# Where four bilinear corners are added in 240 of the 576 sampling steps: by VectorE, or by TensorE in accumulating transposes

## The reference

```
val = g00 * (1 - wy1) * (1 - wx1) + g01 * (1 - wy1) * wx1 + g10 * wy1 * (1 - wx1) + g11 * wy1 * wx1
val = val * mask[:, None]
out = jnp.einsum('bckhw,ock->bohw', val, weight.reshape(weight.shape[0], C, KK))
```

## Time and profile before

| what | value |
|---|---|
| median of 3 runs | 8815.93 us (8812.18 to 8817.9) |
| profiled execution, its own time | 8820.57 us |
| its span, first to last instruction | 8818.8 us |
| first gather of iteration 1, 2, 3, and of the final stage | 1375.0, 3312.8, 5248.2, 7175.9 us |
| VectorE busy | 5978.0 us (68%) |
| GpSimd busy | 5508.2 us (62%) |
| TensorE busy | 4891.3 us (55%) |
| ScalarE busy | 2531.7 us (29%) |

### The profile page before, as it was taken

One profiled execution on the slowest core, in us unless ns is written; L12 is line 12 of the kernel. 1 busy time (PEld: TensorE's weight loads), 2 busy tenths in 40 slices (PEclk: granted clock), 3 DMA queues, 4 the chain that ended last, 5 costly groups with the idle time before them and its releaser, 6 DMA issues. The chain is left out here.

```text
span 8818.8 us, 80494 instructions
## 1 busy us (share of the span) xinstructions
PE 4891.3 (55%) x23346; PEld 2932.9 (33%) x23346; DVE 5978.0 (68%) x6782; ACT 2531.7 (29%) x4248; POOL 5508.2 (62%) x5206
## 2 busy tenths in 40 slices
PE   4555675657766556667756566577755632222222
PEld 3333323434433234434433234344433321111111
DVE  5688557778885767778875767788875654444444
ACT  1355331235532312245522312244512300000000
POOL 0000005768877657768877657778877667777776
PEclk9877887778878777778877777788877865555555
DMA  2000033333333543333333533333333533333333
GB/s 77 22 0 0 22 89 110 106 108 91 91 114 107 163 133 102 106 106 90 91 118 107 168 126 105 102 105 90 90 120 106 167 115 112 113 113 113 112 113 104
DMA packets 443193, 887.45 MB, mean 101 GB/s; under 512 B 119073, under 2 KB 268919, under 8 KB 439925
## 3 DMA queue, kind: packets, MB, share of 16 engines
q0 software_dynamic: 248832, 679.81, 26.4%
q1 hardware_dynamic: 190708, 129.65, 5.1%
q10 hardware_dynamic: 3456, 75.50, 2.1%
HBM read 763.04 MB, written 121.53 MB: 100 GB/s over the span
## 5 line engine op out<-in xcount | busy, mean ns | idle before, releaser
L657 POOL DMA_INDIRECT gathered_corners<-gather_table,metas x5184 | 5499.9, 1061 | 3290.0 <-issue 2852.2
L1367 PE MATMUL ps<-ident,sampled 128*128 128x128 f32 (+1 forms) x2160 | 480.8, 375 | 2381.0 <-DVE sampled L745 1273.5
L1124 ACT COPY sampled_by_channel<-ps 128x512 f32<-128x512 f32 x576 | 335.8, 583 | 3370.5 <-PE ps L1367 3130.2
L1444 PE MATMUL ps<-region,woff 128*128 (+2 forms) x3456 | 1232.7, 516 | 23.3 <-ACT region L1109 23.3
L1367 PEld LDWEIGHTS ps<-ident,sampled 128*128 128x128 f32 (+1 forms) x2160 | 319.1, 181 | 2603.0 <-issue 2080.7
L728 DVE TENSOR_TENSOR gathered_corners<-gathered_corners,ps 128x2304 f32<-128x2304 f32 x288 | 735.5, 2554 | 439.4 <-DMA gathered_corners<-gather_table,metas 430.9
L1444 PEld LDWEIGHTS ps<-region,woff 128*128 128x128 f32 x3456 | 689.6, 203 | 521.3 <-issue 100.1
L1351 PE MATMUL ps<-sampled_by_channel,w 128*64 128x256 f32 x2880 | 682.0, 459 | 0.0
L1364 PE MATMUL ps<-ident,weighted_corners 128*128 128x128 f32 (+1 forms) x2880 | 422.8, 313 | 405.5 <-DVE weighted_corners L726 405.5
L739 DVE TENSOR_TENSOR ps<-gathered_corners,ps 128x1152 f32<-128x1152 f32 x144 | 196.2, 1363 | 653.7 <-DMA gathered_corners<-gather_table,metas 652.4
L1364 PEld LDWEIGHTS ps<-ident,weighted_corners 128*128 128x128 f32 (+1 forms) x2880 | 388.3, 158 | 464.7 <-issue 249.5
(11 more groups left out here) (222 smaller groups left out, 8535.2 us busy)
## 6 DMA issues: line engine op xcount, KB each, us to landing
gathered_corners<-gather_table,metas POOLq DMA_INDIRECT x5184
x_after_layer<-region ACTq DMA_DIRECT2D x8, 4608.0 KB, 14.6
gather_table<-tabst SPq DMA_DIRECT2D x192, 192.0 KB
region<-in_x_dram ACTq DMA_DIRECT2D x12, 1536.0 KB, 10.8
region<-x_after_layer ACTq DMA_DIRECT2D x4, 4608.0 KB, 14.7
res<-x_after_layer SPq DMA_DIRECT2D x144, 128.0 KB
out_dram<-ob SPq DMA_DIRECT2D x144, 128.0 KB
indices_and_weights<-region SPq DMA_DIRECT2D x16, 810.0 KB
```

Source lines behind the costliest of these rows:

```text
L657: pool.indirect_dma_start(out=G[:, s % NG, k, :], out_offset=None, in_=table, in_offset=bass.IndirectOffsetOnAxis(ap=idx[:, s * KK + k:s * ...
L1124: nc.scalar.copy(VT[:, i, 0:4, 128 * t2:128 * t2 + 128], ps[:, 5, :].rearrange("p (k n) -> p k n", k=4))
L1367: mm = pe.transpose(out_m, V[:, s % 2, 128 * m:min(128 * m + 128, KK * C)], ident[:, :])
L1444: mm = pe.matmul(out_rows[:, top:bottom, left:right], woff[:, e, k, :], rhs, start=n == 0, stop=n == KK - 1)
```

## The change

In 20 of the 36 groups (0 to 9 and 22 to 31) both engines' `steps_of` lose their argument `False`, so that they take the form with `sum_on_pe`. That is 80 steps in each iteration and 240 in all. The last four groups of an iteration and the final stage keep their forms. The code of the three forms is untouched.

```
-                    steps_of(c, slot, (0,), False, first)
+                    steps_of(c, slot, (0,), first=first)
...
-                    steps_of(c, slot, (2,), False)
+                    steps_of(c, slot, (2,))
...
-                    steps_of(G_NORM, G_NORM % 2, NORM_PLACES.get(c, ()), False)
+                    steps_of(G_NORM, G_NORM % 2, NORM_PLACES.get(c, ()))
...
-                        steps_of(j + G_CONV[0], (j + G_CONV[0]) % 2, CONV_PLACES[e], False)
+                        steps_of(j + G_CONV[0], (j + G_CONV[0]) % 2, CONV_PLACES[e])
...
-                        steps_of(j + G_COSINES, (j + G_COSINES) % 2, COSINE_PLACES[e], False)
+                        steps_of(j + G_COSINES, (j + G_COSINES) % 2, COSINE_PLACES[e])
...
-                    steps_of(c, (0,), False)
+                    steps_of(c, (0,))
...
-                    steps_of(q // 3 + G_CONV[0], CONV_PLACES[q % 3], False)
+                    steps_of(q // 3 + G_CONV[0], CONV_PLACES[q % 3])
```

More of the change, by code:

```diff
@@ L806, in chunk @@
                         ch.named(ch.after().tensor_tensor(ek4[:, i], kps, wide(kmax[:, i]), ALU.subtract), k_sub, c * 2 + (i + 1))
-                    steps_of(c, slot, (1,), False, first)
+                    steps_of(c, slot, (1,), first=first)
                     for i in range(2):
@@ L836, in chunk @@
                             ch.named(ins, at_cp, c + 1)
-                    steps_of(c, slot, (3,), False)
+                    steps_of(c, slot, (3,))
                     if not last:
@@ L864, in _ @@
                 repeat_edges(pad2_1, 2, PAD2)
-                steps_of(G_NORM, G_NORM % 2, (2, 3), False)
+                steps_of(G_NORM, G_NORM % 2, (2, 3))
                 v.wait_ge(x1_stored, 16)
@@ L992, in _ @@
                     for e in range(12):
-                        steps_of(j + G_CONV[1], (j + G_CONV[1]) % 2, SUM_PLACES[e], False)
+                        steps_of(j + G_CONV[1], (j + G_CONV[1]) % 2, SUM_PLACES[e])
                     ch.restart()
@@ L997, in _ @@
                         t = j * 12 + e
-                        steps_of(j + (G_CONV[1] + 2), (j + G_CONV[1]) % 2, SUM_PLACES[e], False)
+                        steps_of(j + (G_CONV[1] + 2), (j + G_CONV[1]) % 2, SUM_PLACES[e])
                         v.wait_ge(c2_mm, t + 1)
@@ L1401, in _ @@
                         mm.then_inc(q_mm, 1)
-                    steps_of(c, (1,), False)
+                    steps_of(c, (1,))
                     for i in range(2):
@@ L1414, in _ @@
                         mm.then_inc(m_mm, 1)
-                    steps_of(c, (2,), False)
+                    steps_of(c, (2,))
                     pe.wait_ge(m_cp, c * 2 + 2)
@@ L1428, in _ @@
                     mm.then_inc(y_mm, 1)
-                    steps_of(c, (3,), False)
+                    steps_of(c, (3,))
                 group_mean(1, oct_avg[:, :])
-                steps_of(G_NORM, (0, 1), False)
+                steps_of(G_NORM, (0, 1))
                 group_mean(2, pair_avg[:, :])
@@ L1460, in _ @@
                     offset_bank(0, 0, b)
-                    steps_of(G_NORM, ((), (2,), (3,), ())[b], False)
+                    steps_of(G_NORM, ((), (2,), (3,), ())[b])
                 for e in range(2):
@@ L1497, in _ @@
                         mm.then_inc(c2_sum, 1)
-                        steps_of(j + G_CONV[1], SUM_PLACES[e], False)
+                        steps_of(j + G_CONV[1], SUM_PLACES[e])
                 pe.wait_ge(c2_copied, RT + 4)
@@ L1505, in _ @@
                                   start=True, stop=True).then_inc(c2_mm, 1)
-                        steps_of(j + (G_CONV[1] + 2), SUM_PLACES[e], False)
+                        steps_of(j + (G_CONV[1] + 2), SUM_PLACES[e])
                 group_mean(4, pair_avg[:, :])
@@ L1524, in _ @@
                         mm.then_inc(n_tr, 1)
-                        steps_of(j + G_COSINES, COSINE_PLACES[tile], False)
+                        steps_of(j + G_COSINES, COSINE_PLACES[tile])
                 pe.wait_ge(cos_cp, RT + 2)
```

## The result

The changed kernel takes 8691.51 us (median of 4 runs, 8684.81 to 8698.38) against 8814.06 us before (4 runs, 8811.01 to 8817.9): a ratio of 0.9865, 95% interval 0.9851 to 0.9878. That is 122.5 us less, where the interval stands for 107 to 131. The forecast was 8685 us, 129 less than 8814, in a range of 8640 to 8750.

What follows compares the result with a forecast made beforehand. GpSimd's gathers were taken as the bound; 104 us from longer gathers, 9 from L817 and 24 from waits sum to 137 us off 8820.6, or 8683.6 us. Allowing for the runs' median and unsure terms it said 8685, range 8640 to 8750.

Steps and rivals of the forecast that it cites:

- What bounds the kernel: GpSimd's gathers are the bound, floor 45.1 us a group of 36; layer 0's nine groups take 432.0 us.
- Longer gathers: Layers 0 to 2 and cosines: gathers no longer held up by VectorE's two-SBUF-operand adds; 34.5 us an iteration, 104 in three.
- L817: Layer 0: this VectorE instruction comes 2.25 us earlier against the gathers; 0.3 us a chunk gained, 9 us over 27 chunks.
- pairs of L730 and L733: The removed VectorE adds, two operands in SBUF, lengthen gathers: 0.44 us a pair in layer 0, 0.4 in the cosines.
- Waits of GpSimd: GpSimd's waits for a free buffer shrink as it is released 2.25 us earlier: 8.0 us an iteration, 24 us.
- so it gives +0.7 to -0.9: Chain to the cosines' start, step 29.3: turn starts 2.25 us sooner but lasts 1.6 to 3.2 us longer.
- group 29's wait of 3.14 us: GpSimd's wait in layer 2's second half, 2.84 us over the ordinary gap, shrinks by 2.25 us.
- Group 9: Normalized map ready 4.5 us sooner, longer turns of steps 9.2 and 9.3 cost 3.3 us; net -1.2, bounds -5 and +2.
- TensorE at nothing in layer 0: Longer turns fit TensorE's slack, 37 to 43 us of work a chunk; costed at nothing, at most 103 us over 27 chunks.
- Rival A: TensorE becomes the bound in layer 0, clock staying at 1.2 GHz, 58 us a chunk against 48; about 9040 us; chance 0.05.
- Rival B: Longer gathers stay, their overlap with the adds being chance or any VectorE work; only waits go, 8797 us; chance 0.05.
- C: Half the gain: other VectorE instructions catch the gathers, or first tile and cosines lose it; 8745 to 8780 us; chance 0.13.

Runs made afterwards that it cites:

- e1: Changed kernel plus two idle VectorE adds of the old sizes, both operands in SBUF, after the buffer release in the 240 changed steps: 8819.5 us.
- e2: Changed kernel plus two idle VectorE products of the old sizes, one operand of each in PSUM, after the buffer release in the 240 changed steps: 8694.0 us.
- e4: Changed kernel with five transposes instead of 20 in the 240 changed steps, leaving three corners out of the sum there: 8634.3 us.
- e3: As e2, but the buffer release and the signal to TensorE both come only after the idle instructions: 8791.2 us.
- e10: As e2, but TensorE is told right after the product while the buffer is released only after the idle instructions: 8697.7 us.
- e5: Changed kernel, but in layer 2's second half TensorE turns a step after the next three tiles' matmuls instead of before them: 8634.9 us.
- e8: The kernel before with the change made only in layer 0's nine groups, 108 of the 240 steps: 8748.6 us.

## Why the prediction was right

*What bounds the kernel* held: GpSimd's gathers, with a floor of 45.1 us a group, reached after the change in the groups shown of both convolutions (45.0, 44.9).

*Longer gathers,* forecast at 104 us, and *L817,* 9 us. I counted in the two traces under which VectorE instruction each gather of over 1 us starts, and by how much they exceed the usual one. Before, 257 gathers start under L730; 248 of them are over 1 us, 117 us longer together, and the other nine start in its last 0.16 us. After, L730 (in groups 32 to 35 alone) costs 16 us: 101 us gained. L817 gave 12 us, and the rest some 7, most of it in layer 1's resampling, which was not changed. None of the 536 gathers that start under L728 is over 1 us. No gather starts under L733, since those that L730 holds up stand until after its end. So the prediction's "pairs of L730 and L733" are L730 alone. The mechanism is shown, not argued: e1 and e2 are 125.5 us apart and differ in the place of one operand and in the operation, and L817 and the final stage rule out the operation.

*Waits of GpSimd,* forecast at 24 us gained: this term is wrong in size and sign, GpSimd's idle time grew by 4 us. The start of layer 1's convolution went as forecast (10.90 us before, 8.49 after). What failed is the account of layer 2's second half. The prediction costed a longer turn against an earlier start at one step, 29.3, "so it gives +0.7 to -0.9". It left out that steps 28.2 and 28.3 have a matmul queued behind the turn in the same way, and that VectorE waits for it before it comes to the next step, so that group 29's wait of 3.14 us, which it counted down by 2.25, went up to 4.70. For groups 28 to 30 its terms for gathers and waits make 10.7 us gained an iteration. Measured were 1.4 with 20 transposes a step and 12.2 with five (e4). So what the prediction had too small there is the cost of the turn's length: 10.8 us an iteration. e3 and e10, e4, and e5 show it from three sides: late turns cost 94 us, short ones give 53, the same ones in another order 48.

*Group 9* was forecast at -1.2 us net of waits, and groups 9 and 10 together are 1.2 us shorter in the second iteration (128.0 and 126.8). This agreement is chance: the gathers there are 2.6 us shorter and the idle time is 1.3 us longer, and over the three iterations the idle time is the same (145.6 and 145.5 us). The turns cost 6.5 us there (e4), where 3.3 were costed.

*TensorE at nothing in layer 0* held: e4 has the same 411.6 us with five transposes. *Rival A* did not come, as the clock rose with the work, from 0.75 to 0.87 in layer 0; its own terms, 8820.6 + 270 - 32, make 9059 us and not 9040. *Rival B* fell with e1 and e2. *C* did not happen either: L817 moved to a better phase, not a worse one.

That the total came so close, 8685 against 8691.5, is in part luck. The forecast's 137 us were for an execution like the profiled one, and the two profiled ones differ by 130.4. Against the forecast, the waits gave 28 us less. The gathers gave 7 us more, and 15 us came from the slower gathers of the one profiled execution before.

## What to carry to other kernels

Where GpSimd's indirect DMAs set the pace, count which VectorE instructions have two operands in SBUF: moving one operand to PSUM, or the work to TensorE, was worth some 120 us here. Giving VectorE its old load back, as e2 does, cost no more than the noise. When work moves onto an engine that runs in program order, look at what is queued right behind it and who waits for that; turning a group after the matmuls that others wait for was worth 48 us here and cost nothing. In this kernel the largest lengthening left is in layer 1's resampling: half of the gathers there take about 1.1 us or more against 0.95 elsewhere, and together they are some 362 us longer than the usual gather, three times what this change gained. That was not tried.

## What the runs showed of the hardware

An indirect DMA (0.95 us by itself) that starts while VectorE runs an add or product with both operands in SBUF ends 0.81 to 0.84 us after that instruction's end: in the six cases shown of three kernels, and in all 248 long gathers under L730 before and all 233 under L748 in e1. The 19 others that start under these two take their usual time; they start in the first 0.04 us of the instruction or the last 0.16. What counts is the instruction that runs when the gather starts. One that begins while the gather already stands (L750 in e1) adds nothing, and gathers that start up to 0.5 us before an L730 or L748 take their usual 0.95 us.

A second form appears in e2: 20 of its gathers had been running for 0.13 to 0.41 us when L800 began, a TENSOR_SCALAR with one large operand in SBUF, and each ended 0.12 us after it. Here is one, GpSimd and then VectorE:

```profile
3419.33 1.34 POOL L657 DMA_INDIRECT gathered_corners<-gather_table,metas  x1 [0.31 <-issue]
...
3419.74 0.81 DVE L800 TENSOR_SCALAR work<-region,small 128x1024 f32 x1 [0.22 <-DVE sampled L751]
```

The Trainium skill, page "SBUF — State Buffer", section "Who interferes with whom", says that instructions with two SBUF inputs contend with GpSimd's reads, and the traces agree. Its inference that descriptor generation is not held up by them does not save these indirect DMAs, as 1.88 us against 0.95 in e1 and e2 show. Whether it is the reading of their indices or the generation of descriptors that stands still, no run separates.

More transposes raised TensorE's clock. In layer 0 the granted clock was 0.75 before, 0.80 with five transposes a step and no adds (e4), and 0.87 with 20. These are the rows of layer 0 in e4 and in e8, which has 20 there:

```profile
3253.20:3664.80 411.60, 261.02 (x1235) 180.08 (x1235) 247.33 (x249) 105.36 (x161) 312.88 (x324) 0.80 0.37 110
```

```profile
3296.60:3707.80 411.20, 295.40 (x1760) 234.06 (x1760) 247.15 (x247) 102.69 (x160) 312.53 (x324) 0.88 0.37 110
```

The level even rose within a turn. These windows of the kernel after the change are 14.7 us without any work of TensorE, then 1 us out of the turn behind it (20 transposes and nothing else, 3.90 us), then that turn's end:

```profile
3713.30:3728.00 14.70, 0.00 (x0) 0.00 (x0) 13.84 (x15) 0.74 (x2) 6.80 (x7) 0.50 0.22 63
3730.10:3731.10 1.00, 1.00 (x6) 1.00 (x5) 0.97 (x2) 0.00 (x0) 0.73 (x1) 0.50 0.99 352
3731.10:3732.00 0.90, 0.90 (x8) 0.64 (x6) 0.87 (x2) 0.00 (x0) 0.87 (x1) 0.93 0.99 410
```

The granted clock went from 0.50 to 0.93 there, from the 1.2 to the 2.4 GHz level. The Trainium skill, page "TensorE: Matmul & The Clock Gate", Part 4, says that the full clock does not engage for transposes. For these float32 transposes the measurement decides otherwise.
